# W1's and W2's stores on two semaphores, three spare early scatters, and a time table with 131 of 311 positions changed

## What is computed

```python
xn = _layernorm(x, axis=-1)
x = x + _L0_attn_ref(xn, ...) + _L0_ffn_ref(xn, ...)      # layer 0
xn = _layernorm(x, axis=-1)
x = x + _L1_attn_ref(xn, ...) + _L1_ffn_ref(xn, ...)      # layer 1

def _L0_ffn_ref(x, Wg, bg, W1, b1, W2, b2):               # E = 8 experts, K = 2 chosen per row
    logits = jnp.einsum('bsd,de->bse', x, Wg) + bg
    _, top_idx = jax.lax.top_k(logits, K)
    sel = jnp.sum(jax.nn.one_hot(top_idx, E, dtype=logits.dtype), axis=-2) > 0
    gates = jax.nn.softmax(jnp.where(sel, logits, -jnp.inf), axis=-1)
    for e in range(E):
        h = jax.nn.relu(jnp.einsum('bsd,dh->bsh', x, W1[e]) + b1[e])
        y = jnp.einsum('bsh,hd->bsd', h, W2[e]) + b2[e]
        out = out + gates[..., e:e + 1] * y
```

## Time and profile before

| | us |
|---|---|
| median of 3 runs | 1731.67 |
| the 3 runs | 1731.02, 1731.67, 1733.10 |
| the profiled execution | 1727.8 |
| its span, first to last instruction | 1725.6 |

### The profile page before, as it was taken

How to read it: one execution, slowest core, us unless ns; L and a number is a source line. 1 busy time by engine, 2 the same in 40 slices (tenths; PEclk the granted TensorE clock), 3 DMA queues, 4 the chain that set the end, 5 groups by cost and what they waited for, 6 DMA issues and landing times.

```text
span 1725.6 us, 33661 instructions
## 1 busy us (share of the span) xinstructions
PE 1518.9 (88%) x11497; PEld 652.6 (38%) x11497; DVE 1181.6 (68%) x3135; ACT 1050.8 (61%) x2322; POOL 790.8 (46%) x725
## 2 busy tenths in 40 slices
PE   3587898899899998999899999999899999889878
PEld 1253453235333543345333543345333533232232
DVE  7454578566886689767975789667985677477522
ACT  2372475667657766677657766677567765726542
POOL 5246346434744446455645456354654462511120
PEclk9997598999999999999999999999999999979987
DMA  7651461136211542236212631145213620201010
GB/s 287 196 160 54 144 168 33 52 99 177 78 46 56 154 114 63 67 88 190 64 40 72 168 103 50 62 118 159 63 41 93 183 79 14 62 13 38 1 37 7
DMA packets 138872, 159.32 MB, mean 92 GB/s; under 512 B 15744, under 2 KB 100304, under 8 KB 137808
## 3 DMA queue, kind: packets, MB, share of 16 engines
q1 hardware_dynamic: 134608, 148.79, 29.8%
q0 software_dynamic: 4096, 8.40, 1.7%
HBM read 115.96 MB, written 40.85 MB: 91 GB/s over the span
## 4 chain that ended last, share of the span: by engine, by line
PE 63%; DVE 14%; ACT 9%; issue 6%; DMA 4%; SPq 2%; POOL 2%; ACTq 0%; DVEq 0%; POOLq 0%
PE banks L467 60%; DVE negmax L892 7%; ACT probs L1236 3%; ACT hm L1305 3%; DMA qkc<-relm 2%; POOL xslots L1431 1%; DVE h L1117 1%; PE banks L744 1%; ACT L1236 1%; PE banks L697 1%; SPq L1593 1%; DVE h L1112 1%; DVE r_b L1142 1%; DMA wexp<-h_lo 1%; DMA relq<-halves 1%
## 5 line engine op out<-in xcount | busy, mean ns | idle before, releaser
L1236 ACT ACTIVATE probs<-banks 128x512 f32<-128x512 f32 (+3 forms) x1216 | 581.6, 535 | 373.9 <-PE banks L467 369.6
L892 DVE TENSOR_REDUCE negmax<-banks 128x1 f16<-128x512 f32 x768 | 492.4, 685 | 139.3 <-PE banks L467 136.2
L888 DVE CUSTOM_DVE_ANT_0 scr<-banks,mask_row 128x384 bf16<-128x384 f32 (+3 forms) x512 | 230.2, 487 | 151.5 <-PE banks L467 149.6
L467 PE MATMUL banks<-kp,qs 32*128 32x512 f16 (+3 forms) x1024 | 242.6, 359 | 56.0 <-DVE negmax L892 23.1
L467 PE MATMUL banks<-probs,vp 128*32 128x512 f32 (+3 forms) x2048 | 238.3, 539 | 0.5 <-POOL probs L1409 0.5
L467 PE MATMUL banks<-qs,kp 32*128 32x512 f16 (+3 forms) x1024 | 210.1, 349 | 17.3 <-ACT probs L1236 12.6
L1497 POOL TENSOR_TENSOR h_lo<-h,h_hi 128x512 f16<-128x512 f32 x96 | 112.8, 1190 | 221.3 <-ACT h_hi L1348 135.6
L1437 POOL TENSOR_TENSOR hl<-hm,hh 128x512 f16<-128x512 f32 x120 | 139.7, 1166 | 158.0 <-DVE hh L1059 158.0
L1305 ACT ACTIVATE hm<-banks,wt 128x128 f32<-128x128 f32 x480 | 137.8, 375 | 70.1 <-PE banks L467 69.8
L467 PE MATMUL banks<-qkc 97*128 97x512 f16 (+1 forms) x512 | 167.7, 400 | 8.6 <-DVE negmax L892 3.0
L467 PEld LDWEIGHTS banks<-kp,qs 32*128 32x128 f16 x1024 | 65.2, 92 | 262.2 <-DVE negmax L892 100.5
(11 more groups left out here) (217 smaller groups left out, 2442.9 us busy)
## 6 DMA issues: line engine op xcount, KB each, us to landing
wt<-wexp SPq DMA_DIRECT2D x120, 258.0 KB, 3.0
wt<-wexp SPq DMA_DIRECT2D x120, 256.0 KB, 3.5
qkc<-relm SPq DMA_DIRECT2D x96, 128.0 KB, 3.3
qs<-relq SPq DMA_DIRECT2D x64, 128.0 KB, 2.5
kp<-relk SPq DMA_DIRECT2D x64, 128.0 KB, 2.7
relm<-halves SPq DMA_DIRECT2D x32, 256.0 KB, 2.2
xg<-xslots SPq DMA_DIRECT2D x24, 256.0 KB, 2.9
yslots<-yv SPq DMA_DIRECT2D x24, 256.0 KB, 3.7
```

Of the source, the lines that this page charges most:

```text
L467: return nc.tensor.matmul(psum[rows_, bank, cols_], lhsT, rhs, start=start, stop=stop)
L888: v.tensor_tensor_reduce(scr[:, s, 0:kw], psum[:, SCO + s, 0:kw], mask_row[:, T - kw:T], -1.0, 3e38, ALU.add, ALU.min, negmax[:, g.n % 2, ...
L892: v.tensor_reduce(negmax[:, g.n % 2, NC * h + c:NC * h + c + 1], psum[:, SCO + s, 0:kw], AX.X, ALU.max, negate=True).then_inc(sem("max"), 1)
L1236: a.activation(keys(g, c)[:, 2 * pair + s, q0:T], psum[:, TRA + s, q0:T], ACT.Exp, scale=SCALE[main(g)]).then_inc(sem("exp"), 1)
```

## The change

It has three parts.

1. `w_kept` becomes two semaphores. The biases' DMA and W1's four add to `w1_kept`, W2's four to `w2_kept`. The first `load_up` waits for the five of `w1_kept`, the first `load_down` for the four of `w2_kept`.
2. GpSimd issues three more indirect DMAs, which write zeros of `kp` to three scratch tensors in DRAM that nothing reads: one behind `x_root` of batch entry 0, two behind its `lat_root`. SP waits for all three before it enters its loop.
3. 131 of the 311 positions in `AT` and 14 entries of `MOVE` have new values. The groups' starts (`PLAN` and the `MOVE` entries that they use) are the same.

```diff
+        cold = [nc.dram_tensor(f"cold{n}", (P, 2 * D), F16, kind="Internal").ap() for n in range(3)]
...
-        STORED_W = 16 * 9
...
+            COLD_AT = {time("x_root", 0): 1, time("lat_root", 0): 2}
...
+                def cold_scatter():
+                    p_.indirect_dma_start(cold.pop(), bass.IndirectOffsetOnAxis(kp[:, 0, 0:2].bitcast(U32), 0),
+                                          kp[:, 0, 0:2 * D], None).then_inc(sem("cold"), 16)
...
                     norms(G)
+                    for _ in range(COLD_AT.get(G, 0)):
+                        cold_scatter()
                     experts(G)
...
-                                     half(n, k).bitcast(F32).rearrange("p (e f) -> p e f", f=256)).then_inc(sem("w_kept"), 16)
+                                     half(n, k).bitcast(F32).rearrange("p (e f) -> p e f", f=256)).then_inc(sem("w2_kept" if n >= 2 else "w1_kept"), 16)
...
                     if n == 0:
-                        sp.wait_ge(sem("w_kept"), STORED_W)
+                        sp.wait_ge(sem("w1_kept"), 5 * 16)
...
                 def load_down(b, t):
                     n = NT * b + t
+                    if n == 0:
+                        sp.wait_ge(sem("w2_kept"), 4 * 16)
...
                 sp.wait_ge(sem("planes"), 96)
+                sp.wait_ge(sem("cold"), 16 * sum(COLD_AT.values()))
```

Of the positions, those that the prediction speaks of (the value before, then after):

```diff
-"q0_send": -27, "k0_send": -10, "ca_o_out": 145, "back1": 181, "ctx": 185, "f3_add": 172, "wo1": 256, "store": 256
+"q0_send": -16, "k0_send": -11, "ca_o_out": 142, "back1": 182, "ctx": 182, "f3_add": 175, "wo1": 257, "store": 257
-("h0", i): (26, 36, 43, 52)      ("spread0", i): (-7, -5, 5, 16)   ("w_store", i): (-3, -3, -3, 2)
+("h0", i): (28, 36, 43, 52)      ("spread0", i): (-10, -7, 2, 14)  ("w_store", i): (-9, -7, -7, 4)
-("wup", i): (5, 7, 7, 9, ...)    ("wdn", i): (8, 12, 13, 14, ...)  ("scatter", i): (-17, -16, -16, -15)
+("wup", i): (6, 6, 7, 11, ...)   ("wdn", i): (7, 10, 11, 15, ...)  ("scatter", i): (-22, -16, -16, -14)
-("warm0", i): (35, 39, 42, 46, 48, 55, 58, 62, 71, 70)    ("warm1", i): (177, 180, 185, 188, 192, 192, 196, 198, 198, 198)
+("warm0", i): (36, 38, 39, 47, 49, 59, 60, 66, 70, 69)    ("warm1", i): (177, 180, 186, 188, 191, 193, 204, 199, 200, 197)
-MOVE: "route": {0: 7}            "warm0": {1: -2, 2: 2, -3: -1, -2: -4, -1: -5}          "warm1": {0: -2, 1: -1, 2: -1, -1: 6}
+MOVE: "route": {0: 8, 1: 1}      "warm0": {0: -2, 1: -4, 2: 5, -3: -2, -2: -7, -1: -9}   "warm1": {0: -1, 1: -3, 2: -1, -3: -4, -2: 1, -1: 9}
```

More of the change, by code:

```diff
@@ L81 @@
 A1_AT = (120, 128, 136, 152)
[L83 to L85 removed]
+MOVE = {"route": {0: 8, 1: 1}, "warm0": {0: -2, 1: -4, 2: 5, -3: -2, -2: -7, -1: -9}, "warm1": {0: -1, 1: -3, 2: -1, -3:
+        -4, -2: 1, -1: 9}, "front": {0: 1}, "keys": {0: -8, 1: -5, 2: 1}, "joined": {0: 3}, "prep": {0: 13},
+        "ca": {-1: -24}, "mid": {-1: -24}, "last": {-1: -30}, "ffn": {-1: -24}, "tail": {-2: -12, -1: -52}}
 @dataclass
@@ L114, in groups_in_order @@
     return out
[L117 to L121, removed]
[3 rows of a table removed]
-      "caq": 77, "caq_out": 78, "caq_low": 78, "caq_send": 79, "cak": 79, "cak_out": 79, "cak_low": 82, "cak_send":
[L126 to L142, removed]
@@ L143 @@
-AT.update({("xg_load", i): at for i, at in enumerate((-7, -5, 6, 19), 0)})
+AT = {"l1_split": -17, "x_load": -59, "x_stat": -50, "x_root": -50, "x_norm": -48, "xT0": -39, "xT0_out": -38, "xr_hi": -40,
+      "xr_lo": -37, "lat": -37, "lat_stat": -37, "lat_root": -35, "lat_norm": -33, "latT": -32, "latT_out": -32, "q0":
+      -35, "q0_out": -33, "q0r": -32, "q0r_out": -31, "q0_sum": -30, "q0_send": -16, "k0": -19, "k0_out": -18, "k0r":
+      -16, "k0r_out": -14, "k0_sum": -14, "k0_send": -11, "rank0": -35, "rank1": -31, "rank2": -32, "gex": -30,
+      "gates": -29, "pos": -30, "starts": -27, "slots": -25, "addresses": -25, "pick": -15, "v0a": 3, "v0a_out": 4,
[3 rows of a table added]
+      "caq": 77, "caq_out": 78, "caq_low": 78, "caq_send": 79, "cak": 79, "cak_out": 79, "cak_low": 82, "cak_send":
+      82, "ca_spread": 109, "cav": 111, "cav_out": 113, "v1": 129, "v1_out": 130, "bo": 102, "ca_div": 136, "ca_mul":
+      140, "ca_o": 142, "ca_o_out": 142, "gelu1": 151, "gelu2": 166, "f3": 171, "f3_out": 173, "f3_add": 175, "back1":
+      182, "ctx": 182, "mcq": 205, "mcq_out": 206, "mcq_low": 207, "mcq_send": 210, "mck": 207, "mck_out": 208,
+      "mck_low": 209, "mck_send": 211, "mc_spread": 211, "mcv": 220, "mcv_out": 221, "mc_div": 249, "mc_mul": 252,
+      "mc_o": 254, "mc_o_out": 255, "ctx2": 255, "wo1": 257, "wo1_out": 257, "store": 257}
@@ new lines @@
+AT.update({("spread0", i): at for i, at in enumerate((-10, -7, 2, 14), 0)})
+AT.update({("spread1", i): at for i, at in enumerate((109, 117, 129, 147), 0)})
+AT.update({("h0", i): at for i, at in enumerate((28, 36, 43, 52), 0)})
+AT.update({("h0_out", i): at for i, at in enumerate((28, 37, 43, 52), 0)})
+AT.update({("h1", i): at for i, at in enumerate((151, 157, 166, 179), 0)})
+AT.update({("h1_out", i): at for i, at in enumerate((151, 157, 167, 180), 0)})
+AT.update({("up", i): at for i, at in enumerate((9, 12, 13, 16, 17, 20, 22, 24, 25, 29, 30, 32, 33, 35, 38), 0)})
@@ new lines @@
+AT.update({("down", i): at for i, at in enumerate((13, 15, 17, 18, 21, 23, 25, 27, 31, 32, 33, 34, 37, 39, 41), 0)})
+AT.update({("wup", i): at for i, at in enumerate((6, 6, 7, 11, 13, 15, 17, 22, 23, 25, 26, 26, 30, 31, 35), 0)})
+AT.update({("wdn", i): at for i, at in enumerate((7, 10, 11, 15, 16, 21, 23, 23, 23, 27, 31, 31, 33, 33, 39), 0)})
+AT.update({("scatter", i): at for i, at in enumerate((-22, -16, -16, -14), 0)})
+AT.update({("gather", i): at for i, at in enumerate((45, 46, 48, 49), 0)})
@@ L152 @@
+AT.update({("warm1", i): at for i, at in enumerate((177, 180, 186, 188, 191, 193, 204, 199, 200, 197), 0)})
 AT.update({("scale", i): at for i, at in enumerate((52, 51), 0)})
-AT.update({("split", i): at for i, at in enumerate((-13, -11, -4, 3, 8, 21, 39), 0)})
-AT.update({("load", i): at for i, at in enumerate((1, 15, 26), 4)})
+AT.update({("split", i): at for i, at in enumerate((-14, -14, -4, 3, 8, 21, 38), 0)})
+AT.update({("load", i): at for i, at in enumerate((1, 15, 24), 4)})
 AT.update({("fa", i): at for i, at in enumerate((133, 135, 137, 139), 0)})
```

26 lines of the change are left out of this document (13 added, 13 removed), and 6 rows, old and new, of the table AT.

## The result

Beside each other on one chip, the changed kernel took 1746.8 us (median of 5, 1739.9 to 1753.3) and the kernel before 1733.1 us (median of 5, 1731.0 to 1736.3). The ratio is 1.0081, 95% interval 1.0062 to 1.0101: **0.8% slower**, where 1723.7 us and a range of 1715 to 1733 were forecast. The profiled execution took 1739.9 us, its span is 1738.2 us at a mean granted clock of 0.946.

The account below looks back on a forecast made before the run. PE was taken to bound the kernel, busy 88% of the span. Terms 1.3 + 2.2 + 2.5 + 2.0 = 8.0 us, so 1731.7 - 8.0 = 1723.7 us, range 1715 to 1733.

Parts of the forecast that it names:

- steady-state term: Position changes in the repeated loop: h0's wait gone, ca_o_out and ctx nearly covered; 2.0 us won, of 11.0 lost to 3.2 won.
- rival C: New waits on ACT and DVE for ca_o_out and ctx uncovered: 11.0 us lost, 5.0 slower overall, 1736.7 us; chance 0.13.
- Spare scatters: GpSimd's first real scatter, warmed by spare ones, ends earlier; one place gained, 1.3 us, bounds 0 and 8.4.
- Rival A: All three long scatters were cold, so scatters land 8.4 us earlier: 14.2 us won, 1717.5 us; chance 0.08.
- Two semaphores: First load_up no longer waits for W2's last part; first weights land at 64.0, not 66.25: 2.2 us, of 0.5 to 3.5.
- Entry 1's scatters: First two scatters move into GpSimd's idle time; PE's wait for layer 1's xn falls 7.0 to 4.5: 2.5 us won.
- the term of `h0`: h0 0 behind max_rows needs the same bank; PE's wait for pack at L744 goes from 3.2 us to near 0.
- three priced terms: Gains forecast for spare scatters, two semaphores and batch entry 1's scatters: 1.3, 2.2 and 2.5 us.
- the prediction's own sign: A new row of ACT r_b, mixa or DVE ctxT among waits with more than 2 us would show uncovered waits.
- Rival B: First two parts do nothing and steady-state waits cancel; only entry 1's 2.5 stay: 3.0 us won, 1728.7; chance 0.19.
- Fillers and the end: Fillers delay PE's last product by 1.0 us, none after the change; another moves between transposed scores: 0, of 1.5 either way.
- the warning: Prediction wrong if the granted clock after 146 us moves; full clock 10 us earlier or later matches any term.

Follow-up runs that it names:

- c_after2: The changed kernel without further edits, run a third time: 1755.5 us beside 1751.1 for the kernel before, ratio 1.0021.
- a_q0r_back: The changed kernel with q0r and q0r_out alone at their old positions: 1729.7 us, ratio 0.9866 to the kernel before.
- r_split_late: The base with DVE's first three long two-input instructions moved behind the small ones of pick: 1726.7 us, one run, beside 1751.1 for the kernel before.
- r_no_spare: The base without the three spare scatters and SP's wait for them: 1731.3 us, ratio 0.9858 to the kernel before.
- b_code_only: The kernel before with the two semaphores and the three spare scatters, its old table whole: 1749.4 us, ratio 0.9981 to the kernel before.
- r_one_wait: The base with the first load_up waiting for W2's stores too: 1733.3 us, ratio 0.9867 to the kernel before.
- r_base2: The base once more, unedited, in the fourth group: 1727.7 us, ratio 0.9854 to the kernel before.
- r_scatter_back: The base with scatters 0 and 3 at their old positions (-17 and -15): 1741.8 us, ratio 0.9933 to the kernel before.
- c_after: The changed kernel without further edits, run again in the second group: 1742.9 us, ratio 1.008 to the kernel before.
- c_before: The kernel before without edits, run again for its trace in the second group: 1736.4 us, one run, beside 1733.4.
- the base: The changed kernel with twelve routing and latent positions back at old values and rank1's four multiplications as one: 1728.1 us, ratio 0.9845 to the kernel before.
- a_rank1_one: The changed kernel, all positions new, with rank1's four multiplications as one instruction: 1726.3 us, ratio 0.9969 to the kernel before.

## Why the prediction was wrong

**The step that failed** is "The other positions shift work by a step or two between the same neighbours, and I see no row that prices them", inside the steady-state term of 2.0 won. The neighbours were not the same: with `q0r_out` one step earlier and `rank1` one later, `r_b` stands ahead of `rank1`, and DVE's multiplications come beside GpSimd's tensor instructions. The borders lose 32.8 us by the two traces, and putting `q0r` and `q0r_out` back is worth 25.8 (c_after2 against a_q0r_back). It is the slower side, but not rival C's mechanism. Rows were there. The earlier trace rows and the earlier trace rows, read together, show DVE holding GpSimd's scatters; I used them for the eight scatters alone. The other direction stands in the trace of the kernel before, one step of the routing ahead of `rank1`, and I did not look at it:

```profile
646.39 1.30 DVE L938 TENSOR_SCALAR gates<-gates 128x32 f32<-128x32 f32 x1
```

```profile
646.47 1.17 POOL L1413 TENSOR_TENSOR halves<-w,halves 128x512 f16<-128x512 f32 x1
```

The same instruction takes 0.18 us at entry 2. It has one input, so two inputs in SBUF are not needed for the hold. What I should have asked of every moved DVE instruction on SBUF is what GpSimd would be doing beside it.

The Trainium skill (SBUF — State Buffer, "SBUF: two separate sides") has the rule that was missing: a DVE instruction with two SBUF inputs and a GpSimd one that reads SBUF take the shared port pair whole, whoever is first, and the other waits for its end. The traces agree on who waits: L931 ends 0.1 us and L933 0.3 us behind GpSimd's tensor instruction, and beside gathers L931 is not held (0.22 us). They do not bear out "whoever is first" by the recorded starts (last section). The other direction, which I had cited for the scatters, the section states for DVE's two-port modes; here the two-input instructions of L1206 and L1211 do it too: r_split_late's 1.01 us against 6.2.

**Spare scatters**: 1.3 forecast, 0.1 us measured at the first real scatter (r_no_spare). The forecast's sign was a spare one near 6 us, and none was slow:

```profile
6.74 1.27 POOL L1525 DMA_INDIRECT cold<-kp  x1 [0.20 <-issue]
15.65 1.04 POOL L1525 DMA_INDIRECT cold<-kp  x1 [0.20 <-issue]
17.00 0.96 POOL L1525 DMA_INDIRECT cold<-kp  x1 [0.30 <-issue]
```

"So the first one was also slow of its own" was wrong. I had compared its start with the split at 30.86 and passed over `l_lo` (L1206, 29.73 to 30.93) just ahead of it, which was running when the scatter began. Rival A falls too, by r_split_late.

**Two semaphores**: 2.2 forecast. The number of the first tile is read at 54 us, its load is issued at 54.57, where about 56 was forecast, and lands at 63.4, where 64.0 was. The chain of the changed kernel, from the first scatter to that load:

```profile
30.27 6.20 POOL xslots L1433
...
47.61 2.23 DMA xslots<-xr,idx
...
54.57 8.85 DMA wt<-wexp
```

The first `up` is 2.8 us earlier than in the kernel before (63.52 against 66.35); b_code_only has 2.3 of it, and r_one_wait gives 3.1. Right in mechanism, a little small.

**Entry 1's scatters**: right. 4.3 us of wait for `xn` where 4.5 was forecast. PE's wait for `pack` at L744 in the earlier trace rows, the term of `h0`, only halves, where near 0 was forecast:

```profile
PE banks L592 <- DVE xn L913: 4.3, 1, 4.3
...
PE banks L744 <- DVE pack L899: 1.6, 5, 0.3
```

**The gains**: undersized. Between the five borders the table wins 14.5 us, where the steady state had 2.0. PE's waits from 300 to 1500 us show where a part is: for `hm` at L697 11.9 us become 4.5, for `h` at L1112 7.1 become 4.1, for `r_b` 2.4 become 0. r_base2 and r_scatter_back both have 4.4 for `hm`, so that one is not the scatters'. Which positions win it was not tried. And up to `ca` of entry 1 the changed kernel is 13.8 us ahead (10.7 by c_after against c_before), where the three priced terms made 6.0; the rest has no run either.

**Rival C**: from 300 to 1500 us ACT does wait 7.5 us in seven times for `ca_o`'s matmul, and DVE 11.3 us ahead of `ctxT`, and the kernel before has neither row. By the prediction's own sign that was rival C, so the sign was a bad one: a_q0r_back keeps these positions and is 1.3% faster than the kernel before.

**Rival B** does not fit: both the semaphores and the scatters of entry 1 did what was forecast, and the borders took it back.

**Fillers and the end**: 0 forecast, 1.9 us lost behind the last group. No filler stands ahead of the last product now, as forecast, but the clock is at the lower level from 1732.6 us on, and the eight matmuls that took 1.05 us in the earlier trace rows take twice that:

```profile
1732.63 2.08 PE L467 MATMUL banks<-wide,ctxT 128*128 128x128 f32 x8 [1.51 <-DVE ctxT L1159]
```

c_before and c_after have the same 1.05 and 2.08. The fillers were not tried alone.

**The range**: 1719 to 1728 was said to come "from the bounds of its terms". Added up, those bounds reach from 19.1 us won to 12.0 lost, 1713 to 1744. The measured 1746.8 is outside both, since the hold was in no term.

**The clock**: the stretch of the earlier trace rows at 0.56 was at 0.78 after the change, and the warning pointed there; c_before had 0.70 in it, so a part of that moves without any change, and the lead over the kernel before grew by only 1.7 us there, from `ca` of entry 0 to `ca` of entry 1. What moved against the kernel was the clock at the borders, behind the idle stretches. How much of the 6 to 8 us of each border is clock and how much the idle stretch was not separated by a run. Bounds from the trace: the five idle stretches are 20.2 us, and 54.6 us at the lower level cost 27.3 at the most, 47.5 together for the 32.8 lost.

## What to carry to other kernels

When a table moves work by one step, ask of every DVE instruction on SBUF, the small ones too, which GpSimd instruction will run beside it: here four of 0.2 us came to cost up to 4.5 us of PE at an entry, and the clock behind it. Put such small work where GpSimd only issues DMAs, and as one instruction where a broadcast allows it, since each can be held anew. A table that is fitted whole can carry one bad pair under good ones: with two of 131 positions undone it is 1.3% faster than the kernel before in place of 0.2% slower, and the base is faster than the kernel before and the changed one, by 1.5% and 1.7% (0.9854, and 0.9854 / 1.0021 = 0.983). All of this is from chips where the kernel before takes 1751 to 1755 us; where it takes 1733, only a_rank1_one ran, 0.3% faster.

## What was not expected of the hardware

The hold reaches back in the records: L933 of a_rank1_one started 0.3 us before GpSimd's instruction, and the second L931 of the changed kernel 0.6 us before, and both were held to its end; GpSimd's starts are rough in a trace. And the level of a chip can hide a defect: where the kernel before took 1751 to 1755 us, the changed kernel lost 0.2%, and 0.8% on the other level. What makes the level is open, and the clock alone does not show it. The old table with the code parts had a granted clock of 0.94 to 0.97 in the 60 us at each border on the slower level, but c_before, on the faster one, had 0.94 to 1.00; from 620 to 680 us, with 0.94 against 0.95, the former still lost 2.2 us to the latter at the border.
